# Cross-attention and a mixture of experts on one core: another order for the filling of the query pipeline

## What is computed

```python
x = x + xattn(layernorm(x), ctx, ctx)
#   q = einsum('bsd,hdk->bhsk', query, Wq) + bq      (k and v likewise, from ctx)
#   attn = softmax(q k^T / sqrt(16)); out = concat(attn v) @ Wo + bo
x = x + ffn(layernorm(x))
#   probs = softmax(x @ router_w.T); the two best experts of each token
#   out += w * (gelu(x @ w1[e].T) @ w2[e].T)
```

## Time and profile before

| | us |
|---|---|
| median of 3 runs | 485.78 (484.83 to 487.31) |
| profiled execution | 485.02 |
| its span | 483.2 |
| PE busy | 401.6 |
| DVE busy | 268.6 |
| ACT busy | 219.2 |
| POOL busy | 202.2 |

### The profile page before, as it was taken

The page is one execution under the profiler, slowest core; times in us unless marked ns, Lnnn a source line. Parts: engine busy times, 40 slices in busy tenths (PEclk is TensorE's granted clock), DMA queues, the critical chain, the costliest instruction groups (busy, mean ns, idle before and its releaser), DMA issues.

```text
span 483.2 us, 8572 instructions
## 1 busy us (share of the span) xinstructions
PE 401.6 (83%) x2733; PEld 336.7 (70%) x2734; DVE 268.6 (56%) x602; ACT 219.2 (45%) x399; POOL 202.2 (42%) x179
## 2 busy tenths in 40 slices
PE   7607679999999998623689999899999999999940
PEld 3305566687687666422489999899999999999930
DVE  3975784575465312369575746545446776664310
ACT  1511154564554454150076565464456767454400
POOL 4692462844603432100613364544544535453321
PEclk9956798999989998955799999999999999999985
DMA  8434555426421110184361634534324474231230
GB/s 242 129 91 106 114 115 116 113 57 148 119 40 50 50 43 23 44 220 152 91 235 42 212 64 114 135 57 117 59 41 129 115 214 67 50 55 24 24 37 11
DMA packets 26165, 46.69 MB, mean 97 GB/s; under 512 B 6576, under 2 KB 20016, under 8 KB 23280
## 3 DMA queue, kind: packets, MB, share of 16 engines
q0 software_dynamic: 8576, 16.56, 18.8%
q1 hardware_dynamic: 14048, 26.84, 17.9%
q10 hardware_dynamic: 3504, 2.83, 2.0%
HBM read 32.31 MB, written 13.91 MB: 96 GB/s over the span
## 4 chain that ended last, share of the span: by engine, by line
PE 70%; DVE 8%; DMA 7%; POOL 5%; issue 5%; ACT 3%; ACTq 0%; DVEq 0%; POOLq 0%; SPq 0%
PE ps_s L1497 20%; PE ps_t L1514 13%; PE ps_t L1517 6%; PE ps_s L1246 4%; PE ps_t L1290 3%; PE ps_c L1209 3%; DMA result<-big,rowtok 2%; DMA big<-rows,gtok 2%; PE ps_t L1287 2%; PE ps_a L1312 2%; PE ps_a L1337 2%; PE ps_a L1310 2%; PE ps_c L1312 2%; PE ps_c L1310 2%; ACT big L607 2%
## 5 line engine op out<-in xcount | busy, mean ns | idle before, releaser
L1497 PE MATMUL ps_s<-xgT,KB 128*128 128x256 f32 x912 | 117.1, 285 | 3.0 <-DVE xgT L1127 3.0
L1497 PEld LDWEIGHTS ps_s<-xgT,KB 128*128 128x128 f32 x912 | 111.8, 191 | 4.2 <-DVE xgT L1127 1.7
L548 POOL DMA_INDIRECT result<-big,rowtok x38 | 67.1, 1766 | 112.6 <-DMA result<-big,rowtok 65.1
L860 DVE TENSOR_REDUCE mx<-ps_s 128x4 f32<-128x616 f32 x64 | 49.4, 796 | 40.8 <-PE ps_s L1246 40.5
L516 POOL DMA_INDIRECT big<-rows,gtok x38 | 42.9, 1129 | 44.0 <-DVE gtok L1104 23.9
L607 ACT ACTIVATE big<-ps_t 128x512 f32<-128x512 f32 x80 | 45.1, 595 | 27.0 <-PE ps_t L1287 16.9
L1514 PE MATMUL ps_t<-KB,HTb 128*128 x160 | 56.2, 395 | 0.0
L1246 PE MATMUL ps_s<-KB 96*128 96x308 f32 x128 | 35.4, 372 | 21.5 <-DMA KB<-qd 16.4
L1514 PE MATMUL ps_t<-KB 128*128 x144 | 50.6, 395 | 0.0
L731 ACT ACTIVATE big<-ps_t,wrow 128x256 f32<-128x256 f32 x38 | 18.0, 474 | 70.3 <-PE ps_t L1517 70.3
L1170 DVE SCALAR_TENSOR_TENSOR big<-ps_t,wrow,big 128x256 f32<-128x256 f32 x38 | 18.3, 483 | 52.3 <-ACT big L731 50.6
(11 more groups left out here) (196 smaller groups left out, 689.4 us busy)
## 6 DMA issues: line engine op xcount, KB each, us to landing
VP<-in_wexp SPq DMA_DIRECT2D x8, 1024.0 KB, 5.5
big<-in_wexp SPq DMA_DIRECT2D x8, 1024.0 KB, 5.8
qd<-big SPq DMA_DIRECT2D x32, 128.0 KB, 2.3
KB<-qd POOLq DMA_DIRECT2D x8, 512.0 KB, 5.1
KB<-qd POOLq DMA_DIRECT2D x8, 256.0 KB, 5.5
result<-x SPq DMA_DIRECT2D x8, 256.0 KB, 3.0
rows<-xn SPq DMA_DIRECT2D x8, 256.0 KB, 3.2
XS<-in_x ACTq DMA_DIRECT2D x1, 1024.0 KB, 5.7
```

Source lines behind the costliest of these rows:

```text
L548: pool.indirect_dma_start(out, bass.IndirectOffsetOnAxis(rowtok[:, u, h:h + 1], 0), ys[:, 2 * (u % 2) + h, :], None, compute_op=ALU.add).t ...
L860: dve.tensor_reduce(mx[:, i, :, 2 * k:2 * k + 2].rearrange("p a b -> p b a"), ps_s[n % 2][:, :, 0:2 * KEYS].rearrange("p b (h k) -> p b h ...
L1497: last = mm(ps_s[j // 4][:, j // 2 % 2, (j % 2) * PAIR:(j % 2 + 1) * PAIR], w1[:, w, k, j * P:(j + 1) * P], xgT[:, u % 2, a, k, :], start= ...
```

## The change

The filling is written out as a list of its own for each engine, and `step` begins with m = 0. In that list:

- Pair 0's queries don't go to HBM. ACT (`first_queries`), POOL (`first_low_queries`) and DVE each copy four blocks of 32 partitions straight into slot 0 of `QS`. `by_memory` counts the uses of a slot that do go by HBM.
- PE does pair 0's queries ahead of the key product. DVE normalises pair 2. Pair 2's queries use the bank `ps_a`, and so do the turned maxima of pairs 0 and 1.
- Of batch 0's keys, the second high copy moves from DVE to POOL (`middle_keys`); DVE keeps the four low copies (`low_keys`). `ones` and `last_keys` move to ACT.
- Batch 1's keys move into step 0: `masked_keys(1, ...)` and `low_keys(1, ...)` between DVE's maxima, `high_keys(1, r)` between ACT's exponentials, `middle_keys(1)` at the end of POOL's step. `last_keys(1)` stands in ACT's step 1. `KM[1]` and `KT` lie behind `Q2` in `big`.
- The values are made between the maxima of pairs 0 and 1. The load of the tokens of pairs 2 and 3 is issued ahead of `bo`, `wo` and `rw`.
- `keep_busy(12)` becomes `keep_busy(17)`, and a `keep_busy(1)` stands behind each of the eight groups of scores of pair 0 and behind the first five of pair 1.

```diff
+            def first_queries():
+                for r in range(4):
+                    act.activation(QS[0:32, 0, 2 * r:2 * r + 2, :], qf[32 * r:32 * r + 32, :, :], ACT.Copy).then_inc(q0_high, 1)
...
+            def first_low_queries():
+                low_queries(0)
+                for r in range(4):
+                    pool.wait_ge(*((q0_low, r) if r else (q_lo_made, 1)))
+                    pool.tensor_copy(QS[32:64, 0, 2 * r:2 * r + 2, :], Q2[32 * r:32 * r + 32, 0, 1, :, :]).then_inc(q0_low, 1)
+                pool.wait_ge(q0_low, 4)
+
+            def middle_keys(b):
+                pool.wait_ge(km_hi, 2 * b + 2)
+                for r in range(4):
+                    if r:
+                        pool.wait_ge(ks_mid, 4 * b + r)
+                    pool.tensor_copy(KS[32:64, b, 2 * r:2 * r + 2, :].rearrange("p g k -> p (g k)"),
+                                     KM[b][32 * r:32 * r + 32, 0, :, :, :].rearrange("p g a k -> p (g a k)")).then_inc(ks_mid, 1)
+                pool.wait_ge(ks_mid, 4 * b + 4)
...
+            for m, loaded in ((1, ld_x0), (2, ld_x1)):
+                dve.wait_ge(loaded, 16)
+                statistics1(m)
+            dve.wait_ge(rstd1_made, 3)
+            dve.wait_ge(xn_made, 4)
+            dve.wait_ge(xnT_psum, 1)
+            for i in range(2):
+                dve.tensor_scalar(xn[:, 0, i, :], xs[:, 4 + i, :], mv1[:, 0, i, 0:1], mv1[:, 0, i, 3:4],
+                                  ALU.subtract, ALU.mult).then_inc(xn_made, 1)
+            dve.wait_ge(qf_made, 1)
+            for r in range(4):
+                dve.tensor_copy(QS[64:96, 0, 2 * r:2 * r + 2, :], qf[32 * r:32 * r + 32, :, :]).then_inc(q0_mid, 1)
...
+            masked_keys(0, 0)
+            masked_keys(0, 1)
+            low_keys(0, range(4))
+            for n in range(4):
+                maxima(0, n)
+            statistics1(3)
+            for n in range(4, 8):
+                maxima(0, n)
+            negatives(0)
+            all_values()
...
+            evac_xnT(0)
+            evac_q(0)
+            first_queries()
+            act.dma_start(xs[:, 8:TILES, :], xv[:, 8:TILES, :]).then_inc(ld_x2, 16)
+            evac_xnT(1)
+            for r in range(4):
+                high_keys(0, r)
+            evac_q(1)
+            evac_xnT(2)
+            ones(0)
+            evac_q(2)
+            last_keys(0)
+            evac_maxima(0)
...
+            next_norm1(1)
+            rstd(2, mv1, var1_made, rstd1_made)
+            first_low_queries()
+            middle_keys(0)
+            low_queries(1)
+            queries_read(1)
+            low_queries(2)
+            next_norm1(3)
+            queries_read(2)
+            maxima_read(0)
+            low_queries(3)
+            next_norm1(4)
...
-            keep_busy(12)
+            keep_busy(17)
...
+            for n in range(3):
+                scores(0, n)
+                if n == 0:
+                    pe.wait_ge(qf_made, 2)
+                keep_busy(1, ps_c)
+            q_product(2)
+            for n in range(3, 8):
+                scores(0, n)
+                keep_busy(1, ps_c)
+            maxima_transposes(0)
+            for n in range(3):
+                scores(1, n)
+                if n == 0:
+                    pe.wait_ge(v_made, 4 + 5 * B)
+                keep_busy(1)
```

More of the change, by code:

```diff
@@ L250, in steps @@
         def steps(step, last_steps=None):
-            for m in range(-4, MACROS if last_steps else MACROS + 2):
+            for m in range(0, MACROS if last_steps else MACROS + 2):
                 step(m, lambda d: 0 <= m + d < MACROS)
@@ L336, in maxima @@
                 sp.dma_start(md[u, :, :], nmT[:, :]).then_inc(md_stored[u], 16)
+            queries(1)
+            queries(2)
+            maxima(0)
+            queries(3)
             def step(m, has):
@@ L904, in statistics2 @@
                 dve.tensor_scalar(mv2[:, u, :, 2], mv2[:, u, :, 1], EPS, None, ALU.add).then_inc(var2_made, 1)
-            loads = {1: ld_x0, 2: ld_x1, 4: ld_x2}
+            masked_keys(0, 0)
[8 more added lines that the diff above has]
+            all_values()
+            for n in range(4):
+                maxima(1, n)
+            dve.wait_ge(ld_x2, 16)
+            statistics1(4)
+            for n in range(4, 8):
+                maxima(1, n)
+            negatives(1)
             def last_statistics(i):
@@ L965, in step @@
                         normalise(m - 1, i)
-                if has(2):
-                    for n in range(3, 5):
-                        maxima(m + 2, n)
-                if m >= 0 and has(5):
-                    statistics1(m + 5)
-                if has(2):
-                    for n in range(5, 8):
-                        maxima(m + 2, n)
+                for n in range(3, 5):
+                    if m == 0:
+                        masked_keys(1, n - 3)
+                    if has(2):
+                        maxima(m + 2, n)
+                if has(5):
+                    statistics1(m + 5)
+                for n in range(5, 8):
+                    if has(2):
+                        maxima(m + 2, n)
+                    if m == 0 and n < 7:
+                        low_keys(1, [n - 5])
+                if has(2):
                     negatives(m + 2)
-                if m in (-2, -1):
-                    last_keys(m + 2)
+                if m == 0:
+                    low_keys(1, [2, 3])
                 if has(-1):
@@ L1356, in router @@
                 last.then_inc(lg_psum, 1)
+            pe.wait_ge(ld_id, 16)
+            xn_transposes(0)
+            pe.wait_ge(ld_q, 16)
+            q_product(0)
+            pe.wait_ge(ld_k, 64)
+            for g in range(GROUPS):
+                for c in range(KC):
+                    last = mm(ps_s[0][:, g, 0:B * KEYS], wk_sb[:, c, g * P:(g + 1) * P], ctx_sb[:, c, :],
+                              start=c == 0, stop=c == KC - 1)
+            last.then_inc(k_psum, 1)
+            xn_transposes(1)
+            q_product(1)
+            xn_transposes(2)
+            pe.wait_ge(ld_v, 32)
+            for b in range(B):
+                value_product(b)
+            for n in range(3):
+                scores(0, n)
+                if n == 0:
+                    pe.wait_ge(qf_made, 2)
+                keep_busy(1, ps_c)
[9 more added lines that the diff above has]
+                keep_busy(1)
+            xn_transposes(3)
+            for n in range(3, 5):
+                scores(1, n)
+                keep_busy(1)
+            q_product(3)
+            for n in range(5, 8):
+                scores(1, n)
+            maxima_transposes(1)
             def last_steps():
@@ L1387, in step @@
             def step(m, has):
-                if m == -3:
-                    pe.wait_ge(ld_v, 32)
-                    for b in range(B):
-                        value_product(b)
                 if has(2):
```

222 lines of the change are left out of this document (110 added, 112 removed).

## The result

| | before | after |
|---|---|---|
| median, us | 484.72 (480.83 to 495.20, 20 runs) | 481.99 (477.56 to 547.01, 20 runs) |
| ratio to before | | 0.9934, 95% interval 0.9905 to 0.9964 |
| profiled execution, span | 483.2 | 480.2 |

The kernel is 3.2 us faster by the ratio. The forecast was 9 us. The direction is right, and the median lies in the range, but at its slow end (482.5).

What follows compares the result with a forecast made beforehand. PE bounds the kernel from step 1, so only the front can give much. Span 483.2 - 11.2 (filling) + 2.5 (step 0) = 474.5, with 1.8 around it 476.3; with the median 0.8 higher, 476.7 was said; range 471.5 to 482.5.

Steps and rivals of the forecast that it cites:

- What bounds: Whole kernel: PE is the bound from step 1, so only the stretch ahead of it can give much.
- signs of being wrong: Late read of pair 1 or 2, half clock in the scores, or step 0 over 17 us.
- First scores, 26.1: Filling: first scores start at 26.1 us against 37.60, a gain of 11.5 us, with DVE last.
- Pair 0, 10.1 us: Filling: from first scores to turned maxima pair 0 takes 10.1 us as before, ending at 36.2.
- Pair 1: Filling: scores start at 38.9 after the HBM read, values fill DVE's wait, end at 49.0 to 49.5.
- Step 0, plus 2.5 us: Step 0 loses 2.5 us to batch 1's keys, nearest to ACT's sum of 2.2; bounds 0 and 4.5.
- upper bound of 4.5: Step 0's worst loss, 4.5 us: ACT's part, and DVE's beyond it with two holds of 0.9.
- Step 1, 0: Step 1 and later: no change, late keys and copies fall into gaps; otherwise up to 3 us.
- Rival (c): Step 0 longer and thinner for PE, clock low through step 1: 489; chance 0.11 including a part within noise.
- (b): Products of ones don't hold the clock, DVE and POOL hold each other's copies up: 4 us, 480.7; chance 0.14.

Runs made afterwards that it cites:

- e7: The changed kernel with pair 3's statistics moved from behind the fourth to behind the third maximum of pair 0; ratio to before 0.9918.
- e2: The changed kernel with more products of ones: 14 ahead of the first scores, others in pair 1 and step 0; ratio to before 0.9884.
- e4: e2 with batch 1's keys moved from step 0 into step 1; ratio to before 0.9822.
- e12: e4 with POOL's step 1 residual and key copies behind DVE's low copies, and pair 3's statistics behind pair 0's third maximum; 470.99 us, ratio 0.9709.
- e10: e2 with ACT's four high copies of batch 1's keys moved to step 1, the last keys to step 2; ratio to before 0.9864.
- e5: e2 with ACT's and POOL's copies of batch 1's keys moved to step 1, the last keys to step 2; ratio to before 0.9888.
- e6: e2 with DVE's low masked parts and low copies of batch 1 moved to step 1, the last keys to step 2; ratio to before 0.9863.
- e13: The changed kernel with one added wait: POOL's residual of step 0 starts behind DVE's low masked parts; ratio to before 0.9817.
- e1: The changed kernel without the 13 products of ones between the groups of scores, the 17 at the start kept; ratio to before 0.9926.
- e14: e12 without products of ones except the 17 at the start and the 14 ahead of the first scores; 469.53 us, ratio 0.9723.

## Why the prediction was right or wrong

**What bounds.** Right: the front was the place, and the round through HBM vanished for pair 0. Step 2 began 6.8 us later than forecast; 3.0 of it arose in the filling, most of that in pair 0, 2.6 in step 0 and 1.1 in step 1. Two of the forecast's own signs of being wrong came: the clock at half in the scores, and a step 0 of over 17 us.

**First scores, 26.1.** Right to 0.8 us, with DVE's low copies last, as forecast. The copies took 3.14 for 2.9, the low masked parts 1.43 for 0.98, both beside POOL.

**Pair 0, 10.1 us.** Wrong: it took 12.5. The step that failed is "It holds eight maxima, statistics and a query product now as then". Before, pair 0 had no statistics among its maxima: they ran at 33.11, ahead of the first scores, and next at 49.20. Now they stand between two maxima with no wait beside them, and e7, which moves them into a wait, is 2.2 us shorter. The clock was worth as much: with the statistics where they are and the clock whole, e2's pair 0 took 10.3 us. In e4 it took 11.5, where the 128x2 operation (0.82 in the row at 35.23) took 1.73 us. With both, e12 took 8.5. I had let the products of ones pay for themselves by the clock. They stand behind the scores, but PE idles 3.5 us ahead of the first, and the clock was at half from 26 on; the query product took 3.19 us instead of 1.89. Up to there e2 differs from the changed kernel only by the 14 products ahead.

**Pair 1.** The read landed at 38.4 (e7), forecast 38.9. But since pair 0 ended late, the values began only at 39.29, instead of filling the wait for the read. This is the same 3 us, not another; from its second group on, pair 1 took 9.6 us (42.53 to 52.08).

**Step 0, plus 2.5 us.** This was the mis-sized term: it was 5.1. The mechanism was known, and stood in my upper bound of 4.5 as "two holds of 0.9" (its terms, 2.2 for ACT, 0.9 for DVE beyond it and 1.8 for the holds, add to 4.9). I took the value nearest to ACT's sum, 2.2, and treated DVE's part as covered. The runs say: ACT's copies 1.0 and POOL's about 0.6 (e10, e5); DVE's part 2.8 (e6), most of it one hold (1.86 us in the changed kernel, 1.71 in e2) and the half-clock query product behind it. With the hold gone, e13's step 0 is 14.4 us, near the forecast's 14.5, though ACT's part in it is smaller than the 2.2 that I had put there. That its median, 475.4, is near the forecast 476.7 is luck: its step 2 begins at 85.11, 3.7 us later than forecast, and what follows took 388.5 us instead of 393.2.

I had looked for holds only at the copies, where the earlier trace rows shows them. The earlier trace rows has 0.98 for the two low masked parts, but nothing of POOL was running beside them there: the row was a price without a neighbour. The kernel before shows the neighbour in step 0 itself. These two rows are in its timeline:

```profile
66.55 1.82 DVE L786 TENSOR_SCALAR mv<-mv 128x2 f32<-128x2 f32 x1
67.04 1.28 POOL L439 TENSOR_TENSOR XS<-XS,bo_sb 128x512 f32<-128x512 f32 x1
```

The 128x2 operation takes 0.17 us elsewhere (at 50.19). Beside POOL's residual it took 1.65 us more, already before the change, and the change put a new and longer instruction into that place.

**Step 1, 0.** It was 1.2 us longer. It is bound by PE, so most of its length follows the clock (PE busy 18.16 us for 17.27, waits 0.6 for 0.3): 17.65 us at 0.92 before, 18.8 at 0.89 after, 16.4 at 1.00 in e10 to e12. The late keys on ACT and DVE cost at most the 0.3 us of waits. Rival (c) named this, a thin end of step 0 and a clock that stays low behind it; 1.2 us of it came, beside the larger part that (c) doesn't name.

**Rivals.** (b) came nearest: the products of ones held nothing, and the two engines held each other up. Its 4 us were placed in the filling, where the holds were under 1 us; they were in step 0. That its 480.7 is near the 481.99 is therefore luck too: 4 us in the wrong place.

## What to carry to other kernels

Before an instruction of VectorE is put into a slot, look at what GpSimd does in that slot, and price it at its worst there; one wait on the engine that has time (here POOL, which waits for transfers anyway) bought 2.7 us in step 0, about 1.0 of it through the clock. A piece of work moved between two others is free only in a gap that the trace shows: behind the fourth maximum the statistics cost up to 2.2 us more than behind the third. Products that are to keep TensorE's clock helped here ahead of the scores (e2) and not behind them (e1), and once the order was right, all but the 17 at the start could be left out.

## What I had not expected of the hardware

- The hold lasted to the end of the other engine's instruction: in six kernels DVE's held masked part ended 0.34 to 0.36 us behind POOL's residual. By the records it can be longer than that instruction. DVE's 0.53 us instruction took 2.39, 1.86 more, beside a POOL instruction of 1.28 us; whether POOL's began earlier than recorded is not shown. In e4 one copy of 0.47 us took 2.26, and one 128x2 operation of 0.17 us took 1.73.
- POOL's transfer issues did not hold DVE's low masked parts up: in e13 these ran at 0.53 us each, from 56.5 to 57.5, beside the issues at 56.1 to 57.2.
- A granted clock of 0.50 for 8 us need not show in the time: e14 had it from 38 to 46 us, e12 had 0.60 there, and pair 1 took 11.2 us in both. Whether a whole clock would have made it shorter is not shown; in e14 DVE waited 1.53 us behind a query product of 3.64 us.
